# Two attention layers whose value products run over four key tiles at a time instead of two

## The reference, cut to what matters

```python
# layer 0                                    # layer 1
scores = einsum('bhqd,bhkd->bhqk', Q, K)     energy = einsum('bhqd,bhkd->bhqk', Q, K) / 4
scores = scores + bias                       energy = where(mask == 0, -1e20, energy)
...
attention = softmax(energy, axis=-1)
x = einsum('bhqk,bhkd->bhqd', attention, V)
```

## Time and profile before

| | us |
|---|---|
| median of 3 executions | 1369.26 (1368.49 to 1371.78) |
| the profiled execution: time | 1372.2 |
| its span in the trace | 1370.4 |
| attention of layer 0, all steps | about 185.7 to 560 |
| attention of layer 1, all steps | about 857 to 1292 |
| PE, DVE, ACT busy over the span | 1241.2, 1019.9, 909.4 |

### The profile page before, as it was taken

One profiled execution on the slowest core, in us unless ns is written; L12 is line 12 of the kernel. 1 busy time (PEld: TensorE's weight loads), 2 busy tenths in 40 slices (PEclk: granted clock), 3 DMA queues, 4 the chain that ended last, 5 costly groups with the idle time before them and its releaser, 6 DMA issues.

```text
span 1370.4 us, 25414 instructions
## 1 busy us (share of the span) xinstructions
PE 1241.2 (91%) x8951; PEld 650.2 (47%) x8952; DVE 1019.9 (74%) x2279; ACT 909.4 (66%) x1083; POOL 256.5 (19%) x199
## 2 busy tenths in 40 slices
PE   7859989999999999779999649999999999999746
PEld 3536634444444446436666411455554555555323
DVE  3317889999999982269999469788888888871666
ACT  2316756667667666447776182899999889998614
POOL 1212203333310000029998141000000000000000
PEclk9969989999999999989999865899999999999875
DMA  4788896666555401106665856143434444300000
GB/s 145 227 252 271 263 232 152 140 172 158 139 137 118 94 2 65 39 1 191 210 209 192 216 136 133 33 89 70 94 67 92 80 79 90 68 2 24 1 0 16
DMA packets 101260, 160.99 MB, mean 117 GB/s; under 512 B 9072, under 2 KB 57712, under 8 KB 100640
## 3 DMA queue, kind: packets, MB, share of 16 engines
q1 hardware_dynamic: 99664, 158.13, 45.3%
q10 hardware_dynamic: 1488, 1.42, 0.4%
HBM read 114.34 MB, written 45.18 MB: 116 GB/s over the span
## 4 chain that ended last, share of the span: by engine, by line
PE 78%; DVE 8%; issue 6%; ACT 3%; DMA 3%; SPq 2%; POOL 0%; POOLq 0%; DVEq 0%; ACTq 0%
PE PS L559 17%; PE PS L514 17%; PE PS L546 16%; PE PS L282 7%; PE PS L291 6%; PE PS L538 4%; DMA Pz<-in_ctxT 2%; PE PS L945 2%; PE PS L816 1%; ACT Pz L679 1%; SPq L451 1%; PE PS L419 1%; PE PS L876 1%; DVE Pz L602 1%; ACT Pz L681 1%
## 5 line engine op out<-in xcount | busy, mean ns | idle before, releaser
L681 ACT ACTIVATE Pz<-PS 128x1024 f32<-128x1024 f32 x488 | 483.8, 1019 | 144.4 <-PE PS L546 143.9
L602 DVE CUSTOM_DVE_ANT_0 Pz<-PS,Tz 128x512 bf16<-128x512 f32 x512 | 334.8, 689 | 75.9 <-PE PS L514 75.6
L514 PE MATMUL PS<-Kz,Qz 96*128 96x512 bf16 x1024 | 368.9, 401 | 19.7 <-DMA Qz<-q_parts 11.1
L546 PE MATMUL PS<-Qz,Kz 99*128 99x256 bf16 x2048 | 330.1, 275 | 5.8 <-ACT Pz L679 3.0
L599 DVE TENSOR_REDUCE mx<-PS 128x1 f32<-128x512 f32 x448 | 289.6, 687 | 13.8 <-PE PS L514 13.1
L559 PE MATMUL PS<-Pz,Vz 128*17 128x256 f32 x4096 | 271.5, 383 | 0.2 <-ACT Pz L681 0.2
L546 PEld LDWEIGHTS PS<-Qz,Kz 99*128 99x128 bf16 x2048 | 195.1, 98 | 132.4 <-issue 15.0
L514 PEld LDWEIGHTS PS<-Kz,Qz 96*128 96x128 bf16 x1024 | 99.7, 98 | 179.6 <-DVE mx L602 69.3
L559 PEld LDWEIGHTS PS<-Pz,Vz 128*17 128x17 f32 x4096 | 94.2, 96 | 141.3 <-issue 50.1
L685 ACT ACTIVATE PS<-Tz 128x1024 f32<-128x1024 bf16 x120 | 123.4, 1028 | 3.8
L538 PE MATMUL PS<-Tz,identb 128*128 128x512 bf16 x272 | 104.8, 385 | 3.9 <-ACT Pz L681 3.7
(11 more groups left out here) (218 smaller groups left out, 1244.9 us busy)
## 6 DMA issues: line engine op xcount, KB each, us to landing
k_parts<-Pz SPq DMA_DIRECT2D x192, 128.0 KB
Kz<-k_parts SPq DMA_DIRECT2D x64, 384.0 KB, 4.8
v_ones<-Pz SPq DMA_DIRECT2D x32, 544.0 KB, 4.6
Vz<-v_ones SPq DMA_DIRECT2D x64, 272.0 KB, 6.1
Pz<-in_ctxT SPq DMA_DIRECT2D x32, 512.0 KB, 4.2
Kz<-k_parts SPq DMA_DIRECT2D x64, 256.0 KB, 5.6
Kz<-k_parts SPq DMA_DIRECT2D x64, 128.0 KB, 5.9
Pz<-in_mask_pieces SPq DMA_DIRECT2D x16, 512.0 KB, 7.0
```

The source lines that it names most:

```text
L514: e.matmul(PS[:, unit_bank(L, k, u) if bank is None else bank, :], Qz[0:ROWS, o:o + 128], Kz[b][0:ROWS, hh, c * CH:c * CH + CH], start=Tru ...
L546: m = e.matmul(PS[:, bank, o:o + T], Kz[b][0:KROWS, hh, i * 128:i * 128 + 128], Qz[0:KROWS, q:q + T], start=(L == 0), stop=True, skip_grou ...
L602: e.tensor_tensor_reduce(junk[:, u % 3, :], ps, masks[:, tt, c * CH:c * CH + CH], 1.0, LOWEST, ALU.add, ALU.max, to).then_inc(sem("at_seen ...
L681: m = e.activation(probs(i), PS[:, 2 * (i % 2):2 * (i % 2) + 2, :].rearrange("p a n -> p (a n)"), ACT.Exp)
```

## The change

The value products of a pair no longer stand behind each pair. They stand behind every second pair (j odd), for the four tiles 2j - 2 to 2j + 1 in one run. As the exponentials of up to four tiles now wait for their products while two more are made, the probabilities get six buffers in place of four, and all counts on `at_pv` start from six credits. The two buffers added lie where the mask pieces were staged, which move up in `Pz`; in layer 1 the first exponential therefore waits for the quantized feed-forward weights (`wq_done`), which are staged in the same place, and for the stored keys and values. POOL waits for the last mask piece, its own work, before layer 1's keys and values begin.

The diff, cut to its core (the other places only write `PROBS` for 4 in a wait on `at_pv`):

```diff
+PROBS = 6
+RUN = 4
...
-        def probs(i):
-            return Pz[:, 1024 * (i % 4):1024 * (i % 4) + 1024]
+        def probs(n):
+            return Pz[:, 1024 * (n % PROBS):1024 * (n % PROBS) + 1024]
...
-        maski = [Pz[:, 4096 + 1024 * s:5120 + 1024 * s].bitcast(I32) for s in range(2)]
+        maski = [Pz[:, 6144 + 1024 * s:7168 + 1024 * s].bitcast(I32) for s in range(2)]
...
-                             probs(i)[:, hh * T:hh * T + T], start=(i == 0), stop=(i == NT - 1),
+                             probs(at_count(L, k, NT, i))[:, hh * T:hh * T + T], start=(i == 0), stop=(i == NT - 1),
...
-                for part in range(2):
-                    at_pe_values(e, L, k, 2 * j + part)
+                if (2 * j + 2) % RUN == 0:
+                    for i in range(2 * j + 2 - RUN, 2 * j + 2):
+                        at_pe_values(e, L, k, i)
...
+                if L == 1 and i == 0 and k == 0:
+                    e.wait_ge(sem("wq_done"), 3)
-                if i == 2 and k == 0:
+                if i == (2, 0)[L] and k == 0:
...
-            e.sem_inc(sem("at_pv"), 4)
+            e.sem_inc(sem("at_pv"), PROBS)
...
             pool.wait_ge(sem("at_ocopied"), 2 * NG + 2)
+            pool.wait_ge(sem("mask_done"), 16)
```

More of the change, by code:

```diff
@@ L482, in at_load @@
             for q in range(4):
-                e.wait_ge(sem("at_pv"), at_step(L, g, b, NT, QT * (q + 1) + 4 - 2 * NT))
+                e.wait_ge(sem("at_pv"), at_step(L, g, b, NT, QT * (q + 1) + PROBS - 2 * NT))
                 at_load_keys(e, L, g, b, q)
@@ L660, in at_act_out @@
             g, b = divmod(k, 2)
-            e.wait_ge(sem("at_pv"), at_count(L, k, NT, NT + 4))
+            e.wait_ge(sem("at_pv"), at_count(L, k, NT, NT + PROBS))
             if L == 1:
@@ L675, in at_act_step @@
                         e.wait_ge(sem(f"kv_vstored{s}"), 16 * (NCH // 2 * (L + 1) + 1))
+                to = probs(at_count(L, k, NT, i))
                 if L == 0 and i < 3:
@@ L678, in at_act_step @@
                         e.wait_ge(sem("at_biased"), at_count(0, k, 6, 2 * i + half + 1))
-                        m = e.activation(probs(i)[:, half * 512:half * 512 + 512], PS[:, 2 * (i % 2) + half, :], ACT.Exp)
+                        m = e.activation(to[:, half * 512:half * 512 + 512], PS[:, 2 * (i % 2) + half, :], ACT.Exp)
                 else:
-                    m = e.activation(probs(i), PS[:, 2 * (i % 2):2 * (i % 2) + 2, :].rearrange("p a n -> p (a n)"), ACT.Exp)
+                    m = e.activation(to, PS[:, 2 * (i % 2):2 * (i % 2) + 2, :].rearrange("p a n -> p (a n)"), ACT.Exp)
                 m.then_inc(sem("at_exp"), 1)
@@ L1203, in step @@
                 link(e, i_)
-            e.wait_ge(sem("at_pv"), NT * (4 * NG - 1) + 4)
+            e.wait_ge(sem("at_pv"), NT * (4 * NG - 1) + PROBS)
             step(e.memset(zeros, 0.0))
@@ L1504, in _ @@
             at_load_all_and_masks(sp)
-            sp.wait_ge(sem("at_pv"), NT * (2 * NG - 1) + 4)
+            sp.wait_ge(sem("at_pv"), NT * (2 * NG - 1) + PROBS)
             for name, to in (("wk1", wk[1]), ("wv1", wv[1]), ("win", win), ("wx", wx), ("wout", wout)):
@@ L1544, in _ @@
             at_load_all(sp)
-            sp.wait_ge(sem("at_pv"), NT * (4 * NG - 1) + 4)
+            sp.wait_ge(sem("at_pv"), NT * (4 * NG - 1) + PROBS)
             for name, to in (("tm_val", wval1), ("tm_rec", wrec1), ("tm_out", wout1)):
```

## The result

| | before | after |
|---|---|---|
| median of the executions | 1369.38 us (1368.49 to 1371.78) | 1441.24 us (1432.67 to 1442.06) |
| the profiled execution, and its span | 1372.2, 1370.4 us | 1440.67, 1438.9 us |
| ratio, 95% interval | | 1.0503 (1.0478 to 1.0528) |

The change makes the kernel 5% slower. The forecast was 1429, so its direction and kind were right and its size was 12 us short.

A forecast was written before the change was run, and what follows sets the result against it. PE was taken to set the pace, with DVE close behind in layer 0 and ACT in layer 1. 1372.2 + 36.5 (layer 1) + 23.5 (layer 0) = 1432.2, lowered to 1429 for the median; range 1393 to 1440 us.

The forecast's parts named there:

- The edges of a run: PE loses about 0.09 entering and 0.10 leaving each value-product run; merging two saves 0.20 us per two pairs, 26 us.
- Layer 1's walk: PE waits for ACT's mask and odd exponential; two pairs grow from 6.56 to 7.22 us, eight steps +36.5 us.
- Layer 0's walk: PE waits for DVE and its three banks; two pairs grow from 5.98 to 6.46 us, the layer +23.5 us.
- the other six pairs: Layer 0's pairs outside the five double pairs of a step: from 17.43 to 18.2 us, 0.75 more.
- Parts at nothing: Waits at layer 1's first exponential, mask pieces, key and value loads, and waits for probability buffers would add no time.
- the eighth steps: Last step of each layer, without units: 1.5 us more taken in layer 0, 4.6 in layer 1.
- The clock rival: PE's idles drop the clock to 1.2 GHz for a tenth of 900 us: about +60, or 1490 us; chance 0.04.
- The fast rival: Edges go and engines catch up between runs, ACT's mask being there by 2.43: 1343 us; chance 0.09.

The follow-up runs named there:

- half_max: Layer 0's maxima over half the columns, on the changed kernel with runs of two or of four there: 1365.29 and 1369.75 us; two pairs 5.89 and 5.69.
- split_runs: Changed kernel with value products in runs of one tile, two runs a pair, 256 more runs than before: 1425.94 us (1.0399).
- l1_no_act_mask: Changed kernel, runs of four in layer 1 alone, ACT's mask copy for its even tiles from 2 on left out: 1377.03 us (1.0037).
- half_max_four: Changed kernel, runs of four in layer 0 and two in layer 1, layer 0's maxima over half the columns: 1369.75 us (0.9970).
- room_only: Changed kernel with runs of two again, keeping six probability buffers, the moved mask pieces and added waits: 1370.89 us against 1370.0 (1.0002).
- filled: Changed kernel plus 15 unread matmuls a layer where PE waits for ACT in steps seven and eight: 1432.47 us (1.0442).
- first_pairs: Changed kernel with runs of four only in pairs 0 and 1 of each layer 0 step, runs of two elsewhere: 1379.24 us (1.0059).
- l1_units_moved: Changed kernel, runs of four in layer 1 alone, units there at (0, 1, 3) in even and (2, 2, 0) in odd pairs: 1454.59 us (1.0605).

## Why the prediction was right, and where it fell short

**The edges of a run** (0.31 in, 0.31 out, 0.20 saved for two pairs, 26 us in all): right. `half_max` shows 0.20, `split_runs` 0.22 for each added run. As forecast, the new waits outweighed it: against the saving alone two pairs lose 0.68 us in layer 0 (6.46 for 5.98 less 0.20) and 0.85 in layer 1 (7.21 for 6.56 less 0.20).

**Layer 1's walk**: 7.22 forecast, 7.21 measured; even scores at 3.00 forecast, 3.09 measured; the odd tile's mask matmul at 3.95 forecast, 3.94 measured; a step of 57.9, measured 58.0. That ACT's mask copy holds the even scores is shown by `l1_no_act_mask`.

**Layer 0's walk**: 6.46 forecast, 6.46 in four of the five double pairs and 6.53 in one; waits before the units near the run as walked; the other six pairs 18.2 forecast and measured; a step of 50.5, measured 50.47. That DVE and three banks do it is shown by `half_max_four`. DVE's hole came out as 0.86, forecast 0.85.

**Parts at nothing**: right, by `room_only` for the buffers, the mask pieces and the added waits with runs of two. For runs of four, layer 1's first step grows by the same 4.6 as the next ones, so the waits at its first exponential add nothing there either.

**The step that was mis-sized** is the eighth step of either layer, with layer 0's seventh. The prediction took 1.5 and 4.6 for the eighth steps and 3.15 for the seventh; the trace has 5.8, 9.0 and 4.9, in sum 10.5 us more. `filled` splits it: at least 7.3 us are the clock; of the other 3.2 up to 1.7 are too, and the rest is waits that were rounded away (a step without units was not walked, though it stood in the profile). Against that, the first step of layer 0 shows 0.1 in place of 3.15. The 3 us are there: from the start of the run that ends pair 1 to the end of the step the changed kernel takes 46.1 us and the kernel before 43.1. But what lies ahead of that run swings from kernel to kernel: among the kernels with whole maxima it starts at 187.0 to 189.8 us in the five that begin with a run of four, at 188.1 to 190.1 in the six that have the order of before in layer 0, and the kernel before was profiled at 190.1. So the two misses cover each other in part by luck. With them, the other steps are some 1 us over the forecast: 10.5 - 3.1 + 1.1 = 8.5.

**The range** ended at 1440, and the median of 1441.24 is just over it in microseconds; as a ratio to the kernel before it is inside (1.0503 against 1440 / 1369.26 = 1.0517).

**The clock rival** had been given 0.04 and was thought of as all or nothing, over a tenth of the attention. It came, in a form that was not listed: in the changed kernel only at the ends of the layers, where PE has neither units nor enough projection work to do, and beside the forecast's mechanism rather than in its place. In its steps with units, where PE also idles in every two pairs, the granted clock stayed at 1.00. That is no rule for such steps: it fell in two of them in `first_pairs` and in the third and sixth of `l1_units_moved`. (The price was worked out on 900 us of attention; there are 809 before and 877 after.) The Trainium skill, TensorE: Matmul & The Clock Gate, section on PSUM-queue depth-cycling, was cited for short idles that make the clock swing: in 1008.97 to 1066.97, with idles of 0.5 us in every two pairs, this trace disagrees; round 530 us, with idles of 1.48 and 1.29 us close to each other, the clock did fall, and in `first_pairs`, with 0.37 and 1.06, it fell in two steps and not in four that have the same waits.

**The fast rival** fell at the point that it named: ACT's mask was there at 3.0 and not at 2.43.

## What to carry to other kernels

A longer run of one kind of work saves its switches only if the other engines have enough stored to last through it. So walk one period with every engine's buffers, all of them: the room that counts was PSUM (two tiles of scores, three banks of units) and not the buffers of probabilities, which the change raised from four to six. And walk the first and last iterations too, since there the filling work is missing, the waits are longer, and TensorE's clock can fall on top.

## What the runs showed of the hardware

Fifteen matmuls a layer with no use made the kernel 9 us faster, 1441.2 to 1432.5, by keeping the granted clock at 1.00 where it had been 0.67 and 0.72 for 12 us. In `first_pairs` the same waits of PE left the clock at 1.00 in four steps (48.2 us in the first two of them) and not in two others (49.8 and 49.7). A run of value products in four column groups starts 0.31 us after the last unit of full width and the next unit 0.31 after its last round, where units follow each other by 0.22: 0.09 and 0.10 us at its edges, whether the run has 8, 16 or 32 records.
